# Convolution-and-attention block with a mixture feed-forward: feed-forward products in twos, and products of zeros ahead of the gate

## The reference, cut to what matters

```python
x = x + conv_attention(group_norm(x))      # 4 images of 64 channels x 16 x 16, full attention, 4 heads of 32
t = to_tokens(x)                           # 4 x 256 tokens of 64 values
t = t + attention(layernorm(t))            # causal, 4 heads of 16
xf = layernorm(t)                          # the feed-forward's input
gate_logits = xf @ Wg + bg                 # [1024, 8]
top_w, top_i = top_k(gate_logits, 2); top_w = softmax(top_w)
w_dense = sum(one_hot(top_i, 8) * top_w)   # 2 of 8 weights per token are not zero
for e in range(8):                         # but every expert is computed for every token
    h = gelu(xf @ W1[e] + b1[e])           # 64 -> 256
    out += w_dense[:, e] * (h @ W2[e] + b2[e])   # 256 -> 64
t = t + out
```

## Time and profile before

| | us |
|---|---|
| median of 3 runs | 123.01 |
| lowest and highest | 122.45, 124.1 |
| the profiled execution | 123.65 |
| its span in the trace | 120.6 |
| PE busy in the span | 104.9 |
| DVE busy | 74.1 |
| ACT busy | 65.2 |
| POOL busy | 20.1 |

### The profile page before, as it was taken

The page is one execution under the profiler, slowest core; times in us unless marked ns, Lnnn a source line. Parts: engine busy times, 40 slices in busy tenths (PEclk is TensorE's granted clock), DMA queues, the critical chain, the costliest instruction groups (busy, mean ns, idle before and its releaser), DMA issues.

```text
span 120.6 us, 2236 instructions
## 1 busy us (share of the span) xinstructions
PE 104.9 (87%) x821; PEld 51.0 (42%) x821; DVE 74.1 (61%) x214; ACT 65.2 (54%) x121; POOL 20.1 (17%) x35
## 2 busy tenths in 40 slices
PE   5946987989899999898999998679999999999930
PEld 2323465664565555465667554551322222222100
DVE  5097379969613559999767689987284224414240
ACT  0405974171788756743539778945536555464600
POOL 7900482000000000000000000000037144124400
PEclk9999999999999999999999999985999999999995
DMA  1910003990000000000000000000000000000003
GB/s 30 230 17 2 0 7 106 228 197 4 0 5 0 0 8 0 0 0 0 5 0 5 0 0 0 0 3 0 0 0 5 0 0 0 0 0 0 0 0 87
DMA packets 6073, 2.83 MB, mean 23 GB/s; under 512 B 4000, under 2 KB 6064, under 8 KB 6064
## 3 DMA queue, kind: packets, MB, share of 16 engines
q1 hardware_dynamic: 5104, 2.19, 9.2%
q10 hardware_dynamic: 960, 0.52, 1.9%
HBM read 2.45 MB, written 0.26 MB: 22 GB/s over the span
## 4 chain that ended last, share of the span: by engine, by line
PE 64%; DVE 17%; ACT 9%; DMA 4%; issue 3%; DVEq 0%
PE bank L913 15%; PE bank L924 13%; PE bank L857 6%; PE bank L790 5%; PE bank L822 4%; DMA x<-in_x_dram 4%; PE bank L871 3%; PE bank L841 3%; PE bank L732 3%; PE bank L741 3%; DVE mx L577 2%; DVE mx L573 2%; ACT sq L393 1%; DVE xn L552 1%; ACT sq L398 1%
## 5 line engine op out<-in xcount | busy, mean ns | idle before, releaser
L472 ACT ACTIVATE hid<-bank,b1c 128x1024 f32<-128x1024 f32 x16 | 17.8, 1115 | 16.9 <-PE bank L913 16.9
L913 PE MATMUL bank<-xn,w_sb 64*128 64x512 f32 x64 | 19.4, 694 | 0.0
L430 ACT ACTIVATE pr<-bank 128x1024 f32<-128x1024 f32 (+1 forms) x16 | 14.0, 914 | 8.5 <-PE bank L828 5.1
L924 PE MATMUL bank<-hid,w_sb 128*64 128x512 f32 x64 | 17.3, 618 | 0.2 <-ACT hid L472 0.2
L692 DVE SCALAR_TENSOR_TENSOR yw<-bank,b2c,wc 128x512 f32<-128x512 f32 x8 | 6.0, 747 | 17.3 <-PE bank L924 17.3
L362 POOL TENSOR_TENSOR acc<-yw,x 64x512 f32<-64x512 f32 x1 | 1.3, 1260 | 70.4 <-DVE yw L692 70.4
L913 PEld LDWEIGHTS bank<-xn,w_sb 64*128 64x128 f32 x64 | 5.3, 196 | 12.4 <-issue 11.6
L708 PE MATMUL bank<-still 128*128 128x512 bf16 (+1 forms) x31 | 8.3, 429 | 2.3 <-DVE still L486 1.3
L367 POOL TENSOR_TENSOR acc<-acc,yw 128x512 f32<-128x512 f32 x6 | 7.6, 1273 | 14.9 <-DVE yw L692 14.9
L573 DVE TENSOR_REDUCE mx<-bank 128x4 f32<-128x1024 f32 x8 | 9.3, 1220 | 1.1 <-PE bank L790 1.0
L790 PE MATMUL bank<-k,q 32*128 32x256 f32 (+1 forms) x128 | 8.3, 373 | 1.3 <-ACT q L418 0.6
(11 more groups left out here) (148 smaller groups left out, 175.5 us busy)
## 6 DMA issues: line engine op xcount, KB each, us to landing
w_sb<-in_L_ffn_W_dram SPq DMA_DIRECT2D x3, 512.0 KB, 7.4
x<-in_x_dram ACTq DMA_DIRECT2D x1, 256.0 KB, 3.9
x<-in_x_dram SPq DMA_DIRECT2D x1, 256.0 KB, 5.0
bqkv<-in_L_attn_b_qkv_dram SPq DMA_DIRECT2D x12, 0.1 KB, 1.5
wo1t<-in_L_attn_W_out_dram SPq DMA_DIRECT2D x8, 4.0 KB, 1.6
out_dram<-acc SPq DMA_DIRECT2D x1, 128.0 KB, 2.5
out_dram<-acc ACTq DMA_DIRECT2D x1, 128.0 KB, 2.9
wq<-in_L_conv_w_qkv_dram ACTq DMA_DIRECT2D x1, 96.0 KB, 4.6
```

The costliest lines, as they stand in the source:

```text
L430: nc.scalar.activation(pr[:, b, 2 * p:2 * p + 2, 0:n], two(key, 0, n), ACT.Exp, scale=SCALE[l]).then_inc(free(key), 1)
L472: nc.scalar.activation(hid[:, k % 3, :, :], two(("h", 0, k)), ACT.Gelu, bias=b1c[:, k:k + 1]).then_inc(free(("h", 0, k)), 1)
L913: i = mm(ps(key, i=s), w1_sb[r, e, P * j:P * j + P], XN[r, 2 * s:2 * s + 2, :].rearrange("p b t -> p (b t)"), start=True, stop=True)
L924: i = mm(ps(key, p0=C * s, p1=C * s + C), w2_sb[:, k, :], hid[:, k % 3, s, :], start=(j == 0), stop=(j == FT - 1))
```

## The change

Three things are changed. The first is the order on PE in the feed-forward: two ups, then two downs, with the transposes behind down(1). The second is what that order needs: tiles h go round three places (banks 0-1, 2-3, 4-5), y alternates between banks 6 and 7, and hid has four buffers. The third is that `gate` issues 2, 2, 4 and 4 products of zeros (images 0 to 3) into its own bank, behind its claim and ahead of its wait for XN.

```diff
     for k in range(NK):
-        take(("h", 0, k), 2 * (k % 2), 2)
+        take(("h", 0, k), 2 * (k % 3), 2)
     take(("gate_t", 0), 7)
     for e in range(E):
-        take(("y", 0, e), 4 + e % 4)
+        take(("y", 0, e), 6 + e % 2)
...
-        hid = sb("hid", [P, 3, 2, HALF])
+        hid = sb("hid", [P, 4, 2, HALF])
...
             def gelus(k):
                 filled(act, ("h", 0, k))
-                if k >= 3:
-                    e, j = divmod(k - 3, FT)
+                if k >= 4:
+                    e, j = divmod(k - 4, FT)
...
             def gate(l, b):
                 key = ("logits", l, b)
                 claim(pe, key)
+                idle(key, (2, 2, 4, 4)[b])
                 pe.wait_ge(S["xn", l], b + 1)
...
             up(0)
             up(1)
             pe.wait_ge(ld["w2"], 16)
-            for k in range(NK):
-                if 2 <= k + 1 < NK:
-                    up(k + 1)
-                if k == 1:
+            for e in range(E):
+                if e + 1 < E:
+                    up(FT * e + 2)
+                    up(FT * e + 3)
+                down(FT * e)
+                down(FT * e + 1)
+                if e == 0:
                     key = ("gate_t", 0)
                     claim(pe, key)
                     pe.wait_ge(gsteps, 7)
                     for j in range(TH):
                         i = nc.tensor.transpose(ps(key, P * j, P * j + P), wd[:, j, :, :].rearrange("p q c -> p (q c)"), ident[:, :])
                     i.then_inc(full(key), 1)
-                down(k)
```

More of the change, by code:

```diff
@@ L471, in gelus @@
                         act.wait_ge(hused, e + 1)
-                nc.scalar.activation(hid[:, k % 3, :, :], two(("h", 0, k)), ACT.Gelu,
+                nc.scalar.activation(hid[:, k % 4, :, :], two(("h", 0, k)), ACT.Gelu,
                                      bias=b1c[:, k:k + 1]).then_inc(free(("h", 0, k)), 1)
@@ L923, in down @@
                 for s in range(2):
-                    i = mm(ps(key, p0=C * s, p1=C * s + C), w2_sb[:, k, :], hid[:, k % 3, s, :],
+                    i = mm(ps(key, p0=C * s, p1=C * s + C), w2_sb[:, k, :], hid[:, k % 4, s, :],
                            start=(j == 0), stop=(j == FT - 1))
```

## The result

| | before | after |
|---|---|---|
| median, us | 122.75 (122.45 to 124.1, 4 runs) | 118.09 (116.64 to 118.2, 4 runs) |
| ratio, 95% interval | | 0.957 (0.947 to 0.968) |
| the profiled execution | 123.65 | 116.64 |
| its span | 120.6 | 114.9 |
| time around the span | 3.05 | 1.74 |

The kernel became faster by 4.3%. The forecast was 118.7 with a range of 117.6 to 120.6. So the direction held, and the gain was put too small. The ratios leave out the longest executions, which ran slow, and before has more of those than after: over the 46 executions of before whose span was recorded the median is 124.05, over the 10 of after 118.09.

What follows compares the result with a forecast made beforehand. PE was taken to bound the feed-forward. The terms 2.89 + 0.43 + 1.66 - 0.27 = 4.71 us less gave 118.94 for the profiled execution, 118.3 for the median, taken as 118.7; range 117.6 to 120.6.

Steps and rivals of the forecast that it cites:

- What bounds the kernel: In the feed-forward PE sets the pace: 2.07 us per step, where ACT needs 1.11 per gelu.
- Part 1, entries: Feed-forward on PE: entries into ups and into downs each fall from 15 to 7, 2.89 us less.
- The 0.43 at the end: Last downs run as one phase, so the 0.38 wait for the last gelu and a 0.05 fresh start go.
- The first rival, exposed weight loads: Inside a feed-forward phase weight loads stay exposed, so only 1.6 of 2.89 comes: 120.0 us; chance 8%.
- Part 2, the opening: Feed-forward start: four ups, down(0), down(1), then transposes; weights wd and banks ready in time, no cost.
- Part 3, the zeros and the clock: At the gates, zeros make the ups start 0.27 us later but keep the clock at 1.00, 1.66 less.
- the term of 0.27 for the zeros: Ahead of the feed-forward, zeros delay gate 0 and the last XN, so ups start 0.27 us later; bounds 0 to 2.59.
- 1.66 less: First two ups at full instead of half clock take 1.91 us in place of 3.57; bounds nothing to 1.66.
- the step from 118.3 to 118.7: Median forecast raised from 118.3 to 118.7 us, because part of the profiled execution's 0.64 offset was probably a clock dip.
- The zeros hold the clock: Forecast took full clock behind the gates; the rival that zeros don't hold it gave 120.5 us, chance 9%.
- The zeros as queue: Rival at the gates: the clock already falls near 76, zeros take 0.43 each and delay the path: 125.3 us; chance 3%.
- The rule on mode changes: On PE, changing tiling mode drains the array, changing tile within a mode does not; about 0.10 at each phase's end.

Runs made afterwards that it cites:

- fours: The changed kernel with its feed-forward in phases of mostly four ups and four downs instead of two: 116.72 us, ratio 0.951; repeated on another chip 116.99, 0.942.
- before_again: The kernel before, unchanged and measured once more: 124.56 us, ratio to its other runs 1.011.
- order_only: The changed kernel without the products of zeros, so only the order in twos with its tiles, banks and buffers: 119.92 us, ratio 0.974 to before.
- fours_mid: fours with four more products of zeros behind the first transposes: 116.40 us, ratio 0.941 to before.

## Why the prediction came out as it did

**What bounds the kernel.** Right. PE set the pace in the feed-forward; with its entries halved the time fell by their price.

**Part 1, entries.** Right, 2.89 in the sum. The phases of after have the forecast lengths within 0.01, and fours, where three more entries of each kind go, gives 1.05 for 1.08. The 0.43 at the end came too: the last downs run without a wait. The first rival, exposed weight loads, is refuted: inside a phase pairs are 0.428 apart at full clock across the boundary of steps, in ups (3.63 - 1.92 for four pairs) and in downs, which use all rows (3.58 - 1.87 for four in fours). By the rule that weight loads overlap only across row groups (the Trainium skill, TensorE: Matmul & The Clock Gate, The mechanism) the time would have been 1.3 longer; the trace does not agree with it, and fits the background buffer that the page allows besides.

**Part 2, the opening.** Right. The transposes found wd ready (ended 82.91, wanted at 84.94), and no bank was late.

**Part 3, the zeros and the clock.** This is the step that failed, in its sizes and not in its mechanism: the term of 0.27 for the zeros measured -0.02, and the dip was priced from one execution. The first made the gain too small by 0.29, the second by an amount that no run gives.
- "The ups start 0.27 later": they start 0.02 earlier on the clock of L502. I had counted DVE's queue from L542 on as without a gap. It had one. First the row of DVE before that follows L542, then rows of PE and DVE from the timeline of after.

```profile
77.17 0.42 DVE L548 SCALAR_TENSOR_TENSOR rs<-bank,rs 128x256 f32<-128x256 f32 x1
```

```profile
75.24 0.51 PE L879 MATMUL bank<-wgate,xn 128*128 128x8 f32 x4
...
75.79 0.18 DVE L619 TENSOR_TENSOR lg<-bank,bgate 128x16 f32<-128x16 f32 x1
...
76.15 0.41 DVE L542 SCALAR_TENSOR_TENSOR xr<-bank,sq 128x256 f32<-128x256 f32 x1
76.48 0.41 DVE L548 SCALAR_TENSOR_TENSOR rs<-bank,rs 128x256 f32<-128x256 f32 x1
```

Shifted by the 0.74 of x, gate 0 starts at 75.98 in place of 75.75, 0.23 late as forecast (0.25). L619 is 0.16 late, L542 0.15, L548 0.05. In before L548 started 0.43 behind L542, when ACT's square was there (77.14), in after 0.33 behind. A start-to-start distance of 0.43 for an instruction that can follow after 0.33 is a wait of 0.10, though the row shows no idle time. Besides, the gate products behind zeros take less here: the last four start at 79.69 in before with the first up 0.51 behind, and in after at 79.00 with the first up 0.44 behind. Why they take less was not tested.
- "1.66 less": true of the execution shown, where one stretch of 3.4 us was at half clock. In others it is two, also at this place (before_again, order_only with 3.04), and a mean over executions should have been the term. How much that mean is was not measured, since the other executions show only their mean clock. What I gave as the bound of a dip, "about 1.7", was the price of one stretch and no bound.

**From the sum to the median.** The profiled execution lay 0.64 over its median, and I put part of that down to a dip. It was the other way: it had one of the highest clocks and shortest spans of before (120.6 against a median of 121.3), and 3.05 around the span, where most executions have 2.0. So the step from 118.3 to 118.7, which cut the expected gain from 4.71 to 4.31, had no ground. Of the 0.7 by which the gain was put too small against what the terms give, 0.27 + 0.02 is the zeros and 0.4 this step. With the terms as measured, 4.90 in the feed-forward and 0.02 from the zeros, the median of 122.75 gives 117.8. The measured median is 118.09 and the ratio gives 117.5; that 117.8 lies between them is partly luck, since the dips and the time around the span move single executions by more than 1 us. The lower end of the range, 117.6, had been drawn from the same reading of the offset and left no room for a second stretch at half clock or for less time around the span.

**The other rivals.** The zeros hold the clock in every profiled execution that has them: 1.00 through gate and feed-forward. The zeros as queue need more than 12 of them at full clock, as twice the zeros shows. The rule on mode changes (the Trainium skill, TensorEngine Tiling (Array Packing), Key Properties) fits: the excess, 0.21 and 0.16, is at changes between ups and downs and not between steps of one kind. How it divides into drain and exposed weight load no run separates.

## What to carry to other kernels

Where PE alternates between products that split the array in different ways, read the start-to-start distance of pairs inside a step and across the change: the difference, times the changes that can be merged, is a gain that here needed only a PSUM tile and a buffer more; the phase lengths came out within 0.01 us. Filling PE's gaps with products of zeros was free here up to twelve, and twelve more cost 2.61 us, the full 0.218 each. Before a clock dip goes into a sum, look at how the granted clock and the span differ over the executions, and not at one profile.

## What the runs showed of the hardware

- The clock dip is not the same in each execution: of the same program some ran 3.4 us at half clock behind the gate, some 6.8, and some had another 3.4 us near 10 us. With four zeros near 9.3 us the order in fours had a mean clock of 0.993 to 1.00 in six of six executions; without them, beside it, 0.964 to 0.989.
- Inside a phase a weight load is hidden: loads of 0.19 us start 0.43 apart with the pairs of products, also across steps. A change from row halves to column halves of the array and back costs 0.16 + 0.21 us.
- The time around the span differs by up to 1 us, between programs and between executions: 1.7 for fours in most executions, 2.45 to 2.75 for the same with nine more zeros near the start, 1.7 or 2.4 for fours_mid, 2.0 or 3.0 for before. What sets it lies outside the trace and stays open.
- The read of x, the same in all kernels, let DVE start at 5.13 to 5.87; that moves the whole span by up to 0.74.
